# Gated cross attention and six local attention layers on one core: inverse softmax sums by a DMA round trip, row maxima one slot earlier, local layers unrolled with weights loaded ahead

## The reference

```
x = x + tanh(g_xattn) * cross(layernorm(x), ctx, ctx, mask)
x = x + tanh(g_ffn)   * layers(layernorm(x))

cross : 16 heads of 8; q = x@w_q + b_q, k = ctx@w_k + b_k, v = ctx@w_v + b_v
        softmax over 1601 keys of q.k/sqrt(8), masked; then @w_o + b_o
layers: 6 times  x = attn(shift_tokens(x)) + x
                 x = ffn(shift_tokens(x)) + x
attn  : 16 heads of 64, l2norm of q and k times q_scale, k_scale, rotary tables,
        windows of 32 queries against their own and the preceding 32 keys, softmax, @Wo
ffn   : layernorm * ln_g + ln_b, @W1 + b1, a * gelu(gate), @W2 + b2 (inner width 341)
```

## Time and profile before

| | |
|---|---|
| three runs, us | 5897.64, 5908.12, 5935.22 (median 5908.12) |
| the profiled execution, us | 5908.96, its span 5907.2 |
| TensorE busy | 5563.4 us (94%) |
| VectorE, ACT, POOL busy | 3640.7, 4018.5, 2651.1 us |
| mean granted TensorE clock | 0.976 |
| cross phase | about 0 to 2095 us |
| local layers | about 2095 to 5907 us |

### The profile page before, as it was taken

One profiled execution on the slowest core, in us unless ns is written; L12 is line 12 of the kernel. 1 busy time (PEld: TensorE's weight loads), 2 busy tenths in 40 slices (PEclk: granted clock), 3 DMA queues, 4 the chain that ended last, 5 costly groups with the idle time before them and its releaser, 6 DMA issues.

```text
span 5907.2 us, 162346 instructions
## 1 busy us (share of the span) xinstructions
PE 5563.4 (94%) x51848; PEld 3300.2 (56%) x51848; DVE 3640.7 (62%) x8009; ACT 4018.5 (68%) x10790; POOL 2651.1 (45%) x2280
## 2 busy tenths in 40 slices
PE   5999999999999969999999999999999999999997
PEld 2444444444444446666666666666666666666665
DVE  3666666666666546665666666666666566666664
ACT  2555555555544548887888788877888788878886
POOL 2211122111211046665666556655666566656663
PEclk9999999999999989999999999999999999999999
DMA  3343333433334133333333333333333333333332
GB/s 79 64 76 59 63 56 72 76 62 63 56 68 70 28 117 98 100 99 101 100 96 100 97 106 97 96 101 106 97 96 97 107 98 95 96 110 97 96 96 79
DMA packets 146289, 512.26 MB, mean 87 GB/s; under 512 B 31996, under 2 KB 48252, under 8 KB 127404
## 3 DMA queue, kind: packets, MB, share of 16 engines
q1 hardware_dynamic: 144300, 506.02, 32.8%
q10 hardware_dynamic: 1536, 0.40, 0.0%
HBM read 223.41 MB, written 30.68 MB: 43 GB/s over the span
## 4 chain that ended last, share of the span: by engine, by line
PE 44%; ACT 12%; issue 5%; DVE 2%; ACTq 0%; POOL 0%; DMA 0%; SPq 0%; DVEq 0%; POOLq 0%
PE b_qk L1433 9%; PE b_c L1474 6%; PE b_o L1392 5%; PE b_pt L1372 5%; ACT probs L1135 5%; PE b_sc L1360 4%; PE b_nv L1408 3%; PE b_qk L1444 3%; PE b_sc L1351 2%; ACT L1174 2%; ACT L78 2%; PE b_c L1504 2%; PE b_nv L1504 1%; ACT ln_n L1100 1%; PE b_c L1479 1%
## 5 line engine op out<-in xcount | busy, mean ns | idle before, releaser
L441 ACT ACTIVATE eT<-b_e 128x512 f32<-128x512 f32 (+1 forms) x1664 | 907.7, 594 | 966.4 <-PE b_e L759 961.0
L1135 ACT ACTIVATE probs<-b_sc,nb,rq 128x96 f32<-128x96 f32 (+1 forms) x3072 | 1324.7, 449 | 21.0 <-DVE nb L1268 19.8
L514 DVE CUSTOM_DVE_ANT_0 junk<-b_s,mq 128x1024 bf16<-128x1024 f32 (+1 forms) x1024 | 1000.4, 991 | 447.6 <-PE b_s L741 422.2
L1063 POOL TENSOR_TENSOR probs<-probs,rsums 128x512 f32<-128x512 f32 (+1 forms) x768 | 716.7, 933 | 716.2 <-DVE rsums L1204 708.2
L1259 DVE TENSOR_REDUCE b_sc<-b_sc 128x4 f32<-128x512 f32 (+1 forms) x768 | 486.4, 633 | 804.7 <-PE b_sc L1360 804.5
L1122 ACT ACTIVATE probsT<-b_pt 128x512 f32<-128x512 f32 x768 | 456.1, 594 | 564.3 <-PE b_pt L1372 558.8
L1433 PE MATMUL b_qk<-xs,weights 128*128 128x256 f32 x3072 | 751.5, 388 | 71.8 <-POOL xs L1055 40.2
L755 PE MATMUL b_e<-mk,identb 128*128 128x512 bf16 (+1 forms) x1664 | 654.6, 393 | 45.7 <-DMA q_op<-mp 34.1
L759 PE MATMUL b_e<-q_op,k_op 75*128 75x256 bf16 (+1 forms) x3328 | 658.5, 280 | 0.0
L1433 PEld LDWEIGHTS b_qk<-xs,weights 128*128 128x128 f32 x3072 | 561.8, 193 | 162.4 <-ACT sq L1149 49.4
L1135 ACT ACTIVATION_READ_ACCUMULATOR probs<-b_sc,nb,rq 128x1 f32 x3072 | 643.5, 209 | 0.9 <-issue 0.9
(11 more groups left out here) (133 smaller groups left out, 8343.8 us busy)
## 6 DMA issues: line engine op xcount, KB each, us to landing
rot_p<-rot_s SPq DMA_DIRECT2D x768, 256.0 KB, 2.4
rkb<-rk_scr SPq DMA_DIRECT2D x192, 512.0 KB, 6.2
k_op<-k_scr SPq DMA_DIRECT2D x576, 100.1 KB
v<-v SPq DMA_DIRECT2D x192, 256.0 KB, 3.7
k_scr<-kp SPq DMA_DIRECT2D x48, 400.2 KB, 3.4
ctxT<-in_ctx SPq DMA_DIRECT2D x17, 800.5 KB, 19.9
weights<-in_ffn_w SPq DMA_DIRECT2D x24, 512.0 KB, 5.3
q_op<-q_scr SPq DMA_DIRECT2D x144, 64.0 KB
```

The source lines that it names most:

```text
L441: nc.scalar.activation(eT[0:n, g % 2, i * 512:(i + 1) * 512], b_e[i][0:n, :], ACT.Exp).then_inc(s["e_ready"], 1)
L514: nc.vector.tensor_tensor_reduce(junk[:, half, 0:n], b_s[u % 2][:, 0:n], mq[:, p, qt, half * 1024:half * 1024 + n], 1.0, LOWEST, ALU.add, ...
L1063: nc.gpsimd.tensor_tensor(pu, pu, rsums[:, u % 2, :].unsqueeze(2).to_broadcast([P, 4, w]), ALU.mult).then_inc(s["pn_ready"], 1)
L1135: last = nc.scalar.activation(probs[:, t, k % 2, 2 * e + h, c0:P], b_sc[:, 512 * e + h * w:512 * e + (h + 1) * w], ACT.Exp, bias=nb[:, k % ...
```

## The change

It makes three edits. In the cross phase the softmax sums are sent to DRAM as they are (four partitions of 1024 numbers), read back spread over 128 partitions of 32 numbers, inverted there in one reciprocal, sent to DRAM and read back into four partitions of `r_row`; TensorE then spreads the inverses over 32 partitions with the same matrix as before, now at slots (0,8) and (0,9), and VectorE multiplies straight from the bank. Also in the cross phase, `TURN` is 6 and ACT issues the maxima at slot `TURN + 2` = 8; the last product of a row and its `keep_u` move behind the first scores of the next row; other uses of `b_p`, ACT's splits and POOL's subtraction (behind `max_parts` in quarter 0) move by a few slots. In the local layers the inner loop is written out (twelve row steps in a straight run), the loop over layers gets the hint, and the scales and the K, Q and V parts of the next layer are loaded, and its tables made, within the last row step A of a layer (`LAST`). The weights' array in DRAM has one more layer of zeros, which the last layer's early loads read.

```
-TURN = 7
+TURN = 6
...
-N_SETX = 2
+N_SETX = 3
...
             if prev:
-                at += [(0, 1, "sums", 0), (0, 2, "sums", 1), (0, 8, "out", 0), (0, 10, "mean_y", 0),
-                       (0, 12, "var_y", 0)]
+                at += [(0, 8, "sums", 0), (0, 9, "sums", 1), (0, 11, "out", 0), (1, 0, "mean_y", 0),
+                       (1, 3, "var_y", 0)]
             if nxt:
-                at += [(0, 3, "k", 0), (0, 4, "k", 1), (0, 5, "k", 2), (0, 6, "k", 3), (0, 9, "mean_q", 0),
-                       (0, 11, "var_q", 0), (1, 1, "q", 0), (1, 3, "v", 0), (1, 5, "v", 1), (1, 9, "v", 2),
-                       (1, 11, "v", 3), (3, TURN, "max", 3)]
+                at += [(0, 1, "k", 0), (0, 2, "k", 1), (0, 3, "k", 2), (0, 4, "k", 3), (0, 10, "mean_q", 0),
+                       (0, 12, "var_q", 0), (1, 2, "q", 0), (1, 4, "v", 0), (1, 8, "v", 1), (1, 10, "v", 2),
+                       (1, 12, "v", 3), (3, TURN, "max", 3)]
...
 (SP, cross phase, right behind the load of xb)
+                    sp.wait_ge(s["u_kept"], count("u_kept", b, 4))
+                    sp.dma_start(sum_scr, u4[DK:P:32, :, :].rearrange("h q t -> h (q t)")).then_inc(s["sum_out"], 16)
+                    sp.wait_ge(s["sum_out"], count("sum_out", b, 16))
+                    sp.dma_start(r_sum[:, :], sum_scr.rearrange("h (x c) -> (h x) c", c=32)).then_inc(s["sum_in"], 16)
+                    sp.wait_ge(s["inv_ready"], count("inv_ready", b, 1))
+                    sp.dma_start(inv_scr.rearrange("h (x c) -> (h x) c", c=32), r_inv[:, :]).then_inc(s["inv_out"], 16)
+                    sp.wait_ge(s["inv_out"], count("inv_out", b, 16))
+                    sp.wait_ge(s["un_ready"], count("un_ready", b, 2, back=1))
+                    sp.dma_start(r_row[DK:P:32, :, :].rearrange("h q t -> h (q t)"), inv_scr).then_inc(s["inv_in"], 16)
...
 (POOL, start)
+            nc.gpsimd.memset(r_row[:, :, :], 0.0).then_inc(set_pool, 1)
...
 (ACT)
-                        if kt == 10:
+                        if kt == TURN + 2:
...
 (VectorE)
-                        if prev and q == 0 and 3 <= kt <= 6:
+                        if prev and q == 0 and kt == 3:
                             b = prev[0]
-                            dve.wait_ge(s["sums_kept"], count("sums_kept", b, 2))
-                            nc.vector.reciprocal(ru[:, kt - 3, :], ru[:, kt - 3, :]).then_inc(s["ru_ready"], 1)
...
+                            dve.wait_ge(s["sum_in"], count("sum_in", b, 16))
+                            dve.wait_ge(s["inv_out"], count("inv_out", b, 16, back=1))
+                            nc.vector.reciprocal(r_inv[:, :], r_sum[:, :]).then_inc(s["inv_ready"], 1)
                         if cur and kt == 0 and q > 0:
                             keep_u(dve, cur, q - 1)
+                        if prev and kt == 0 and q == 0:
+                            keep_u(dve, prev, 3)
...
 (TensorE)
-                        pe.wait_ge(s["u_kept"], count("u_kept", b, 4))
-                        last = nc.tensor.matmul(b_p[:, :], w_sb[:, XW_S:XW_S + P], u4[:, 2 * j:2 * j + 2, :],
+                        pe.wait_ge(s["inv_in"], count("inv_in", b, 16))
+                        last = nc.tensor.matmul(b_p[:, :], w_sb[:, XW_S:XW_S + P], r_row[:, 2 * j:2 * j + 2, :],
...
                             if g:
-                                products(*divmod(g - 1, KT))
+                                products(cur, *divmod(g - 1, KT))
+                        if prev and (q, kt) == (0, 0):
+                            products(prev, 3, KT - 1)
...
-                if cur:
-                    products(3, KT - 1)
...
 (local layers, rows)
-                with hinted_loop(nc, eng, 1, NB // 2 - 1) as i:
-                    b = 2 * i
+                for b in range(2, NB - 2, 2):
                     iteration(row(layer, b + 2, 0), row(layer, b + 1, 1), row(layer, b, 0), row(layer, b - 1, 1))
-                    iteration(row(layer, b + 3, 1), row(layer, b + 2, 0), row(layer, b + 1, 1), row(layer, b, 0))
+                    iteration(row(layer, b + 3, 1), row(layer, b + 2, 0), row(layer, b + 1, 1), row(layer, b, 0),
+                              LAST if b == NB - 4 else None)
...
-            with eng.Fori(1, DEPTH) as layer:
+            with hinted_loop(nc, eng, 1, DEPTH) as layer:
...
 (SP, local layers; the loads in layer_start are gone)
                     for i in range(3):
                         swap(i)
+                        if i == 1 and begin == LAST:
+                            load_scales(layer + 1)
+                            wait_apart(sp, sp_passed, s["qk_done"], count("qk_done", n, 4))
+                            load(PART_K, layer + 1)
...
                     swap(3)
+                    if begin == LAST:
+                        wait_apart(sp, sp_passed, s["qk_done"], count("qk_done", n, 8))
+                        load(PART_Q, layer + 1)
                     wait_apart(sp, sp_passed, s["rk_out"], count("rk_out", n, 32))
...
+                    if begin == LAST:
+                        wait_apart(sp, sp_passed, s["v_done"], count("v_done", n, 4))
+                        load(PART_V, layer + 1)
...
 (POOL, local layers; scale_tables holds the four operations that layer_start had)
+                    if begin == LAST and k == 7:
+                        pool.wait_ge(scales_in, 16 * here[0] + 32)
+                        wait_apart(pool, pool_passed, s["rotc_ready"], count("rotc_ready", A[0], 8))
+                        scale_tables()
```

More of the change, by code:

```diff
@@ L44 @@
 AHEAD = 2
+LAST = 3
 HX, DK = 16, 8
@@ L134, in cross_phase @@
         ru = sb("ru", [P, 4, S])
+        r_sum = sb("r_sum", [P, 32])
+        r_inv = sb("r_inv", [P, 32])
+        r_row = sb("r_row", [P, 4, S])
         t1 = sb("t1", [P, S])
@@ L166, in cross_phase @@
         dma_per = dict(xa_in=16, xb_in=16, x1_kept=16, xn_kept=16, ctx_in=16, m8_in=16, mt8_in=16, kscr_in=48,
-                       qscr_in=48, qop_in=9 * 16, mrow_in=4 * 48)
+                       qscr_in=48, sum_out=16, sum_in=16, inv_out=16, inv_in=16, qop_in=9 * 16, mrow_in=4 * 48)
         s = {n: sem(n) for n in (*per, *dma_per)}
@@ L390, in iteration @@
                         max_parts(row, q)
+                    if nxt and q == 0:
+                        b = nxt[0]
+                        pool.wait_ge(s["khi_ready"], count("khi_ready", b, 1))
+                        nc.gpsimd.tensor_tensor(kf[:, :], kf[:, :], kp[:, 0, :], ALU.subtract
+                                                ).then_inc(s["kres_ready"], 1)
                     if nxt and q == 0:
@@ L451, in iteration @@
                                                      bias=vec[:, XV_BK:XV_BK + 1]).then_inc(s["kf_ready"], 1)
-                        if nxt and at == (0, 7):
+                        if nxt and at == (0, 5):
                             b = nxt[0]
@@ L465, in iteration @@
                             nc.scalar.activation(qp[:, 0, :], qf[:, :], ACT.Copy).then_inc(s["qhi_ready"], 1)
-                        if nxt and at == (1, 4):
+                        if nxt and at == (1, 5):
                             b = nxt[0]
@@ L615, in iteration @@
                         at = (q, kt)
-                        if nxt and at == (1, 0):
+                        if nxt and at == (1, 1):
                             b = nxt[0]
@@ L621, in iteration @@
                                                     ).then_inc(s["xq_ready"], 1)
-                        if prev and at == (1, 3):
+                        if prev and at == (1, 5):
                             b = prev[0]
@@ L627, in iteration @@
                                                     ).then_inc(s["xn_ready"], 1)
-                if cur:
-                    keep_u(dve, cur, 3)
             def keep_u(dve, row, q):
@@ L648, in iteration, with products @@
                 where = uses(cur, nxt, prev)
-                def products(q, kt):
-                    b, p = cur
+                def products(row, q, kt):
+                    b, p = row
                     n = tile_keys(kt)
@@ L939, in layer_start @@
                 here[0] = layer
-                if not isinstance(layer, int):
-                    last = layer * NB - 1
-                    wait_apart(sp, sp_passed, s["qk_done"], count("qk_done", last, 8))
-                    load_scales(layer)
-                    load(PART_K, layer)
-                    load(PART_Q, layer)
-                    wait_apart(sp, sp_passed, s["v_done"], count("v_done", last, 4))
-                    load(PART_V, layer)
             def iteration(A, B, C, D, begin=None):
@@ L1001, in _ @@
             sp.dma_start(out, xT[:, :, :]).then_inc(out_sent, 16)
+            sp.wait_ge(scales_in, 16 * DEPTH + 16)
+            for part in (PART_K, PART_Q, PART_V):
+                sp.wait_ge(part_in[part], 16 * DEPTH + 16)
             sp.wait_ge(out_sent, 16)
@@ L1016, in _, with scale_tables @@
             pool.wait_ge(consts_in, 16 * N_CONSTS)
```

(8 more changed lines are left out.)

44 lines of the change are left out of this document (21 added, 23 removed).

## The result

The changed kernel takes **5968.51 us** (5961.87 to 5969.12) against 5914.75 (5897.64 to 5935.22): ratio **1.0077**, 95% interval 1.0059 to 1.0095, so 0.8% slower. (The quotient of these two medians is 1.0091, within the interval.) That is the case "the same" and inside the wide range of 5795 to 5975 us, but 54 us above the forecast, above its own range of 5865 to 5965, and just above the 5967 from which the prediction counted "slower". The profiled execution took 5969.12 us around a span of 5967.3.

The account below looks back on a forecast made before the run. The prediction took TensorE to set the pace, with 48.5 us of waiting and 66 us of half clock to win. 5909 - 92 - 6 + 126 - 25 + 3 = 5915 us; own range 5865 to 5965, with the cases 5795 to 5975.

Parts of the forecast that it names:

- the same: Whole kernel: no change beyond 1% (59 us) either way; chance 0.58.
- Moved maxima: Cross phase: earlier maxima remove 34 us of TensorE waits and 58 us of half clock, -92 us.
- ACT didn't become the bound: Cross phase, rival: ACT's wait for mp at slot 8 stops TensorE, +81 us, 5996 us; chance 0.12.
- Late product: Cross phase: moving a row's last product removes a 3.3 us wait and part of the turn's 8.1, -6 us.
- Inverse sums: Cross phase: late sums make TensorE wait 3.4 us plus 5 of half clock in each of 15 rows, +126 us.
- rival 2: Cross phase: only sum_in is late, costing 15 x 3 to 5 us instead of 126; 5850 to 5865 us; chance 0.13.
- VectorE's relief is worth zero: Cross phase: removing reciprocals and copies from VectorE gains 0 us, since TensorE hardly waits there.
- Local layers: Local layers: early loads and tables gain 4.9 us at each of five layer changes, -25 us.
- The 6.92 us for the tables and xs: Local layers: one TensorE wait at a layer change, hanging on a late par_a, taken as part of its cost.
- The rkb delay: Local layers: Q's early load delays the broadcast of rkb by 2.8 us, leaving TensorE a 1.9 us wait.
- rival 3: Local layers: the straight run saves 1.3 us in each of 30 inner turns, 39 us, giving 5876; chance 0.05.
- Ends: Start and drain: one more memset costs 0.9 us and four DMAs in the drain 2, +3 us.

Follow-up runs that it names:

- the fairer control: The best run with the inverse sums undone and VectorE's sum work back at the slots of the kernel before; ratio 0.9924 to the kernel before.
- the best run: The changed kernel with the small reciprocal at slot 5 instead of 3 and the store of xn behind q_op; 5816.05 us, ratio 0.983 to before.
- the swapped order: The changed kernel with the store of the sums and its load back sent ahead of k_op[3], xa and xb; ratio 1.0007 to before.
- the kept loop: The kernel before with the change's local layers, but the inner loop kept and only its last turn written out; ratio 0.9995 to before.

## Why the prediction was right in its class and wrong in its sum

**Moved maxima, -92.** The waits went as said (32.0 to 2.7), and ACT didn't become the bound in this kernel. The term was mis-sized: undone alone in the cured kernel, it is worth 40 us by medians and 52 by the two profiles. Of the 34 us of waits 18.6 come back there, in nine places, and of the 58 us of half clock some 36.

**Late product, -6.** No run of its own, but both waits that it should take away are still there: 2.8 us for exponentials, now at L773, and 12.5 us at the turn in place of 8.1. It gained nothing that shows.

**Inverse sums, +126.** The mechanism is right in each step: the store stands behind the k_op loads (10.1 us to land, 2.0 ahead of them), sum_in is quick (1.6, which puts rival 2 out), VectorE stands at slot 3 (6.06 us), TensorE stops some 13 us into the row (12.4 predicted) for 3.65 us (3.4 predicted). The size is wrong: it isn't every row. In the timeline TensorE stops so in rows 1, 2, 4, 6, 8, 10, 12, 14 and 15 (counted from 0), for 1.5 to 5.7 us, and in rows 3, 5, 7, 9, 11 and 13 not at all. These begin behind the turn of the loop, where TensorE is held up anyway: sum_scr is sent 2.4 to 3.5 us into the row against 3.7 to 4.1, and r_sum 9 to 10 us against 12 to 15. The cost was 57 us. And the gain was not zero: "VectorE's relief is worth zero" fails as far as the fairer control tells, which is 55 us slower than the best run, with the moved k copies in it. The busy shares of a stage don't tell it; slot 8 of ACT's order does.

The page of the Trainium skill cited there (DMA: Bandwidth & Descriptors, "Why a DMA increments its semaphore by 16 and not by 1") gave the side on which it came out. That these four rows ran on the engines that the k_op loads fill is what the swapped order fits; no run shows the engines one by one.

**The step that failed** is one that the prediction doesn't have. It doesn't follow xn into its queue: the change brings xn from slot 3 to slot 5 of quarter 1, SP waits for it in order, and k_scr, k_op[0], q_scr and q_op stand behind it, while TURN brings the next row's first scores one slot forward. The price is 86 us, more than any other term that the runs show, and the timeline of before shows everything that was needed: xn_scr at 887.62, q_op at 907.51, and the next row's first scores (slot 7 of quarter 2) at 926.28, 84 us into the row.

**Luck.** That the class came out right is in part luck. The change without this step takes 0.9931, or 5874 us, 41 under the forecast; the 86 us that the prediction doesn't have lifted it to 54 above, and against them stand an inverse-sum wait given at twice its price and maxima given at twice their gain. (A slip besides: rival 2's 15 x 3 to 5 us in place of 126 give 5834 to 5864, not 5850 to 5865.)

**Local layers, -25.** Measured 24 by the ratio (interval 15 to 32), 16 by the medians, 23.6 and 20.2 in two profiles. Inside, the steps were off and cancelled. The 6.92 us for the tables and xs, which the prediction takes for every change, are those of the first alone. At the other four TensorE waits 1.9 to 3.8 us for xs and 3.0 to 4.9 us at the turn of the outer loop, a wait that the prediction doesn't have. TensorE's list from 2700 to 5850 us, in before and in after:

```profile
PE b_qk L1433 <- POOL xs L1055: 19.9, 5, 6.9
PE b_sc L1351 <- issue: 17.0, 4, 4.9
...
PE b_sc L1383 <- issue: 10.0, 5, 2.6
PE b_qk L1465 <- POOL xs L1083: 1.0, 1, 1.0
```

The early loads and tables took 18.9 us of waits away; 7 more went at the turn, and the runs above give those to the straight run and not to the hint. The rkb delay is real: POOL's wait went from 0.44 to 2.7 us, a delay of 2.3 against 2.8 taken. But it leaves 1.0 us of wait at TensorE at one change, not 1.9 at each; the other four have 2.2 to 2.6 us in the turn of the outer loop. The changes gain 34.9 us, and where the prediction says that the straight run saves nothing, its steady rows cost 0.10 us a row, 0.2 in the first layer, some 11 in all. Even so it is 13 us shorter than the kept loop, at the exits and changes: the sign of rival 3, in another place. The first two steps of the first layer are 3.9 us longer than in before, and 34.9 - 11 - 3.9 makes the 20.

**Ends, +3.** They don't show: the drain's wait for r_row is 8.3 us where an 8.8 us wait stood, and the first row starts at 107.07 us where it did at 106.96.

**The sum** from the runs, against 5909: -24 for the layers, -40 for the maxima, -37 for the rest of the cross attention (0.9897 against 0.996: the inverse sums without their wait, the late product, k earlier), +57 at slot 3, +86 for q_op: 5951 in this way and 5914.75 x 1.0077 = 5960 by the ratio, 5969 in the profile.

## What to carry to other kernels

When a producer moves by a slot, walk down the in-order DMA queue past the instruction that waits for it, and write beside each DMA behind it when its reader wants it: the dearest term here was a store that nobody waits for. Put small transfers ahead of a burst of large ones only if the whole chain goes ahead; else let the engine ask two slots later, when the burst has run out. A new wait need not be in every row: where the row begins behind another stall, the stall has paid for it.

## What was not expected of the hardware

Straight code costs this TensorE 0.10 to 0.21 us in a row of 38.29, with the bytes of the two instruction queues up from 2.6 to 6.8 MB in the layers (before against the best run), and yet the turn of the outer loop behind it is short: 2.2 to 2.9 us of "issue", against 3.8 to 4.5 with the inner loop kept. A few microseconds of waits bring long stretches of half clock (1.2 GHz): between 250 and 1900 us TensorE is idle for 98 us at a granted clock of 0.95 in the change, and for 23 us at 0.99 in the best run. The total isn't what counts: with the old sums TensorE is idle for 55 us there, in waits of mostly about 1 us, and has 0.98; with xn's store moved alone it is idle for 43 us, in waits of up to 4.7 us, and has 0.97.
